# A post-norm transformer tower on one core: the scan stage's residual is added in PSUM, and the int8 stage's order on TensorE and its norms are rearranged

## The reference

```python
# L2_ffn, its last step: every expert's output goes back to the token that chose it
out = jnp.einsum('...besd,...btes->...btd', inter, perm)
...
# L3_attn
lam_t = sigmoid(x @ W.T + b);  s = lam_t * s + (1.0 - lam_t) * x
...
# L3_ffn
x_scale = jnp.maximum(jnp.abs(x2).max() / 127.0, EPS)
x_int8 = jnp.clip(jnp.round(x2 / x_scale), -128, 127).astype(jnp.int8)
out = acc_i32.astype(jnp.float32) * x_scale * weight_scale.T + bias
...
h = _layernorm(h + _L2_ffn_ref(h, ...), axis=-1)
h = _layernorm(h + _L3_attn_ref(h, ...), axis=-1)
h = _layernorm(h + _L3_ffn_ref(h, ...), axis=-1)
```

## Time and profile before

| what | value |
|---|---|
| median of 3 runs | 1355.79 us (1352.24 to 1357.06) |
| the profiled execution, its own time | 1355.12 us |
| its span | 1353.5 us |
| mean granted clock of TensorE | 0.95 |
| PE, DVE, ACT, POOL busy | 87%, 59%, 43%, 39% |
| mean DMA | 120 GB/s |

### The profile page before, as it was taken

How to read it: one execution, slowest core, us unless ns; L and a number is a source line. 1 busy time by engine, 2 the same in 40 slices (tenths; PEclk the granted TensorE clock), 3 DMA queues, 4 the chain that set the end, 5 groups by cost and what they waited for, 6 DMA issues and landing times. The chain is left out here.

```text
span 1353.5 us, 25791 instructions
## 1 busy us (share of the span) xinstructions
PE 1179.8 (87%) x9651; PEld 925.3 (68%) x9651; DVE 803.3 (59%) x1850; ACT 582.2 (43%) x1467; POOL 521.6 (39%) x564
## 2 busy tenths in 40 slices
PE   6999996698999999996899999995899999889854
PEld 4666665698999999862455656564677777667533
DVE  4666666321221221377999999994677777522886
ACT  3445542211112122155777777771343444334544
POOL 0111111232333333245688888881212212020757
PEclk9999999799999999999899999997999999889975
DMA  4111100888888888389000000002000040037601
GB/s 143 42 48 40 41 13 13 308 336 346 321 323 330 314 331 322 93 217 249 1 1 1 1 1 1 1 1 82 13 10 13 10 192 1 2 125 266 184 5 59
DMA packets 82716, 162.31 MB, mean 120 GB/s; under 512 B 42976, under 2 KB 61536, under 8 KB 76576
## 3 DMA queue, kind: packets, MB, share of 16 engines
q1 hardware_dynamic: 63504, 114.38, 24.8%
q0 software_dynamic: 10224, 44.05, 8.4%
q10 hardware_dynamic: 8864, 2.23, 0.8%
HBM read 134.28 MB, written 26.35 MB: 119 GB/s over the span
## 5 line engine op out<-in xcount | busy, mean ns | idle before, releaser
L936 PE MATMUL banks<-rowsT,w_up 128*128 128x128 f32 x1716 | 201.8, 278 | 0.2 <-DMA w_up<-in_up_w 0.2
L936 PEld LDWEIGHTS banks<-rowsT,w_up 128*128 128x128 f32 x1716 | 198.6, 195 | 0.5 <-DMA w_up<-in_up_w 0.4
L1457 PEld LDWEIGHTS banks<-ys,ident 128*128 128x128 f32 x1008 | 127.7, 191 | 99.5 <-POOL ys L1837 65.6
L1834 POOL TENSOR_TENSOR ys<-xT_d,q_by_time 128x1024 f32<-128x1024 f32 x63 | 149.3, 2370 | 40.5 <-ACT xT_d L1589 40.5
L1457 PE MATMUL banks<-ys,ident 128*128 128x64 f32 x1008 | 136.3, 290 | 21.5 <-POOL ys L1837 21.4
L1448 PE MATMUL banks<-made,ident 128*128 128x512 f32 x256 | 138.2, 622 | 10.7 <-DVE made L1772 10.5
L1670 ACT ACTIVATE banks<-banks,rate 128x256 f32<-128x256 f32 x256 | 104.0, 444 | 71.9 <-DVE made L1767 71.5
L1105 DVE TENSOR_TENSOR hT<-banks,silu 64x128 f32<-64x128 f32 x39 | 11.0, 283 | 168.3 <-ACT silu L993 168.3
L950 PE MATMUL banks<-w_down,hT 128*128 128x256 f32 x468 | 107.5, 379 | 0.6 <-DVE res L1115 0.6
L878 POOL DMA_DIRECT2D w_down<-in_down_w x39 | 22.6, 579 | 189.8 <-PE banks L950 181.7
L1770 DVE TENSOR_REDUCE banks<-made 128x32 f32<-128x544 f32 x128 | 93.1, 727 | 4.4
(11 more groups left out here) (316 smaller groups left out, 2393.9 us busy)
## 6 DMA issues: line engine op xcount, KB each, us to landing
w_up<-in_up_w SPq DMA_DIRECT2D x39, 1408.0 KB, 6.0
w_down<-in_down_w POOLq DMA_DIRECT2D x39, 768.0 KB, 5.3
inter<-res_x SPq DMA_DIRECT2D x16, 512.0 KB, 3.0
back<-inter SPq DMA_DIRECT2D x15, 512.0 KB, 3.8
patches<-in_patches SPq DMA_DIRECT2D x16, 384.0 KB, 3.3
f<-in_f SPq DMA_DIRECT2D x6, 1024.0 KB, 10.3
ys<-token_rows SPq DMA_DIRECT2D x16, 256.0 KB, 2.8
xn_rows<-xn_all SPq DMA_DIRECT2D x16, 128.0 KB, 1.7
```

Of the source, the lines that this page charges most:

```text
L936: ins = pe.matmul(out[:, m * P:(m + 1) * P], w[:, c, m * P:(m + 1) * P], x[:, c, :], start=(c == 0), stop=(c == 1))
L1457: ins = pe.matmul(o_sum[t % 2], ident[:, :], products[t % 2][:, :, :, n], start=(n == 0), stop=(n == FOLDED - 1))
L1834: pool.tensor_tensor(qs[:, :, :, :], Sc[(t + 1) % 2][:, :, :, :], bcast(qt[:, t, :, :], 2, HD), ALU.mult).then_inc(sem("qs_made"), 1)
```

## The change

Five edits, all in `last_layers`.

1. In `mix_back`, TensorE first multiplies the tile of `H` with the identity into the PSUM bank; the four mixing matmuls then accumulate on it (`start=False`). VectorE's add (`r1`) goes. Statistics and first norm read the PSUM bank. The bank is free for tile t only once the first norm of tile t - 2 has been done.
2. On TensorE, the int8 stage's list is now `turn_q`, `int_sums`, `turn_v`; `turn_v` was first.
3. Odd tiles' third norm: GpSimd makes only root and shift, ScalarE the norm (`odd_third_norm`, at lag 3, last in its tick). Even tiles stay on GpSimd.
4. The semaphore `ln3_done` becomes `third0` and `third1`, one for each parity.
5. The wait for the residual's semaphore moves from `statistics` to its callers.

```diff
                 for t in range(T):
-                    sp.wait_ge(sem("ln3_done"), t + 1)
+                    sp.wait_ge(sem(f"third{t % 2}"), t // 2 + 1)
                     sp.dma_start(io["out"][t * P:(t + 1) * P, :], res_q[t % 2][:, :]).then_inc(sem(f"out{t % 2}"), 16)
...
                     if t >= 2:
-                        pe.wait_ge(sem("added1"), t - 1)
+                        pe.wait_ge(sem("ln1_done"), t - 1)
+                    pe.matmul(mixed_bank(t), ident[:, :], H[:, t, :], start=True, stop=False, skip_group_check=True)
                     for k in range(GPT // 2):
                         at = slice(k * 2 * GROUP, (k + 1) * 2 * GROUP)
-                        ins = pe.matmul(mixed_bank(t)[at, :], perm_t[:, t, at], back[t % BACKS][:, k, :], start=True,
+                        ins = pe.matmul(mixed_bank(t)[at, :], perm_t[:, t, at], back[t % BACKS][:, k, :], start=False,
                                         stop=True, skip_group_check=True, tile_position=(0, k * 2 * GROUP))
...
-                ticks([(2, turn_v), (0, turn_q), (1, int_sums)], 2)
+                ticks([(0, turn_q), (1, int_sums), (2, turn_v)], 2)
...
-                    normed(1, x[t % 4][:, :], r1, t)
+                    normed(1, x[t % 4][:, :], mixed_bank(t), t)
...
+                def odd_third_norm(t):
+                    if t % 2:
+                        act.wait_ge(sem("ln3_shift"), t // 2 + 1)
+                        if t >= 3:
+                            act.wait_ge(sem("out1"), 16 * (t // 2))
+                        act.activation(res_q[1], r3[1][:, :], ACT.Identity, bias=shift[3][1][:, :],
+                                       scale=agg[3][1][:, 1:2]).then_inc(sem("third1"), 1)
...
-                ticks([(0, copy_qT), (1, dequantize)], 1)
+                ticks([(0, copy_qT), (1, dequantize), (3, odd_third_norm)], 3)
...
                 def third_norm(t):
                     root(3, t)
+                    if t % 2:
+                        if t >= 3:
+                            pool.wait_ge(sem("third1"), t // 2)
+                        pool.tensor_scalar(shift[3][1][:, :], agg[3][1][:, 0:1], agg[3][1][:, 1:2], -1.0,
+                                           ALU.mult, ALU.mult).then_inc(sem("ln3_shift"), 1)
+                        return
...
                 def add_back(t):
                     dve.wait_ge(sem("mixed_back"), t + 1)
-                    if t >= 2:
-                        dve.wait_ge(sem("ln1_done"), t - 1)
-                    dve.tensor_tensor(r1[t % 2][:, :], mixed_bank(t), H[:, t, :], ALU.add).then_inc(sem("added1"), 1)
-                    statistics(1, r1, t)
+                    statistics(1, mixed_bank(t), t)
...
                 def add_int(t):
                     dve.wait_ge(sem("v_turned"), t + 1)
                     if t >= 2:
-                        dve.wait_ge(sem("ln3_done"), t - 1)
+                        dve.wait_ge(sem(f"third{t % 2}"), t // 2)
```

More of the change, by code:

```diff
@@ L2327, in last_layers @@
         agg = {n: [sb(f"agg_{n}{p}", [P, 2]) for p in range(2)] for n in (1, 2, 3)}
-        shift = {n: [sb(f"shift_{n}{p}", [P, 1]) for p in range(2)] for n in (1, 2)}
+        shift = {n: [sb(f"shift_{n}{p}", [P, 1]) for p in range(2)] for n in (1, 2, 3)}
         largest = sb("largest", [P, T])
@@ L2546, in normed @@
                     act.wait_ge(sem(f"ln{n}_shift"), t + 1)
-                    act.activation(dst, r[t % 2][:, :], ACT.Identity, bias=shift[n][t % 2][:, :],
+                    act.activation(dst, r, ACT.Identity, bias=shift[n][t % 2][:, :],
                                    scale=agg[n][t % 2][:, 1:2]).then_inc(sem(f"ln{n}_done"), 1)
@@ L2571, in second_norm @@
                 def second_norm(t):
-                    normed(2, H[:, t, :], r2, t)
+                    normed(2, H[:, t, :], r2[t % 2][:, :], t)
                 def copy_qT(t):
@@ L2628, in third_norm @@
                     root(3, t)
+                    if t % 2:
[4 more added lines that the diff above has]
+                        return
                     if t >= 2:
-                        pool.wait_ge(sem(f"out{t % 2}"), 16 * (t // 2))
+                        pool.wait_ge(sem("out0"), 16 * (t // 2))
                     pool.tensor_scalar(res_q[t % 2][:, :], r3[t % 2][:, :], agg[3][t % 2][:, 0:1],
-                                       agg[3][t % 2][:, 1:2], ALU.subtract, ALU.mult).then_inc(sem("ln3_done"), 1)
+                                       agg[3][t % 2][:, 1:2], ALU.subtract, ALU.mult).then_inc(sem("third0"), 1)
                 for b in (*xT, *lam, *y):
@@ L2653, in statistics @@
                 def statistics(n, r, t):
-                    dve.wait_ge(sem(f"added{n}"), t + 1)
-                    dve.bn_stats(stats[n][t % 2][:, :], r[t % 2][:, :]).then_inc(sem(f"ln{n}_stats"), 1)
+                    dve.bn_stats(stats[n][t % 2][:, :], r).then_inc(sem(f"ln{n}_stats"), 1)
                     dve.wait_ge(sem(f"ln{n}_stats"), t + 1)
@@ L2674, in add_scanned @@
                                              op0=ALU.mult, op1=ALU.add).then_inc(sem("added2"), 1)
-                    statistics(2, r2, t)
+                    dve.wait_ge(sem("added2"), t + 1)
+                    statistics(2, r2[t % 2][:, :], t)
                 def scan(t):
@@ L2702, in add_int @@
                     if t >= 2:
-                        dve.wait_ge(sem("ln3_done"), t - 1)
+                        dve.wait_ge(sem(f"third{t % 2}"), t // 2)
                     dve.tensor_tensor(r3[t % 2][:, :], scanned_bank(t), H[:, t, :], ALU.add).then_inc(sem("added3"), 1)
-                    statistics(3, r3, t)
+                    dve.wait_ge(sem("added3"), t + 1)
+                    statistics(3, r3[t % 2][:, :], t)
                 for q in range(QUADS):
```

## The result

| | before | changed |
|---|---|---|
| median | 1354.34 us (7 runs, 1352.12 to 1360.81) | 1363.94 us (7 runs, 1361.29 to 1367.13) |
| ratio | | 1.0053, 95% interval 1.0031 to 1.0075 |
| span of the profiled execution | 1353.5 us | 1360.9 us |
| mean granted clock of TensorE | 0.95 | 0.945 |

The changed kernel is slower, by 7.2 us at the ratio (4 to 10 us by the interval). The medians are 9.6 us apart. The prediction was 1364.8 us. The spans differ by 7.4 us, and two stages account for it.

What follows compares the result with a forecast made beforehand. It took VectorE to bound the scan stage and a TensorE-ScalarE loop the int8 stage. Int8 stage +12.1 and scan stage -3.1 gave +9.0 us, so 1364.8 us against the median of 1355.8, range 1359.5 to 1370.

Steps and rivals of the forecast that it cites:

- The int8 loop: Int8 stage: a TensorE-ScalarE loop of 2.22 us gives way to a serial round of VectorE and TensorE, +13.7 us.
- The forecast of the tick: Int8 stage: six pieces from add to add sum to 3.27 us against 2.22, in 13 intervals.
- The last two intervals between adds: End of the int8 stage: with nothing left to quantise they take 3.0 us instead of 4.3, -1.3 us.
- The ends of the int8 stage: Behind the last add: shift and ScalarE's norm stand in for GpSimd's norm of 1.23 us, -0.3 us.
- The odd norms: Int8 stage: odd tiles' norms on ScalarE cost nothing and bring nothing apart from the shorter end.
- The scan stage: TensorE becomes the bound at 2.93 us a tick, VectorE's falls from 3.33 to 2.88; -3.1 us in all.
- the rule of the Trainium skill: Scan stage: statistics from PSUM cost VectorE some 0.065 us more, so the stage brings 0.2 us less.
- Ten ticks: Steady scan stage: the tick falls by 0.40 us over a stretch of 33.3 us, -4.0 us.
- The start of the scan stage: Ahead of the first `lam_logits`: uncovered `H` matmul at clock 0.50 costs 2 x 0.46, +0.9 us.
- The first: Int8 stage: `turn_q` never waits for VectorE, tick 1.87 us, kernel faster at 1347.8 us; chance 0.06.
- The second: Int8 stage: TensorE's clock is granted in full, tick 2.72 us, total 1357.6 us; chance 0.05.
- The third: Scan stage: matmul of `H` costs 0.86 us or more, the stage gains nothing, total 1368.8 us; chance 0.12.

Runs made afterwards that it cites:

- e3: Kernel before with only the odd third norms moved to ScalarE and the semaphore split by parity; ratio 1.0002 to the kernel before.
- e6: Changed kernel with VectorE's add one tick later (lag 3 for 2) and `turn_v` first again on TensorE; ratio 0.9947 to the kernel before.
- e2: Kernel before with only TensorE's int8 order changed (`turn_v` last); ratio 1.0079 to the kernel before.
- e4: Changed kernel with VectorE's add one tick later in its list (lag 3 for 2); ratio 0.9926 to the kernel before.
- e8: Changed kernel with the matmul of `H` issued twice for each tile; ratio 1.0108 to the kernel before.
- e1: Kernel before with only the residual added by TensorE in PSUM; ratio 0.9966 to the kernel before.
- e5: Changed kernel with only TensorE's int8 order undone (`turn_v` first again); ratio 0.9964 to the kernel before.
- e7: Changed kernel with VectorE's add one tick later and all third norms on GpSimd again; ratio 0.9933 to the kernel before.
- e9: Changed kernel with six more identity matmuls ahead of `turn_q` from the fourth tile on; ratio 1.0018 to the kernel before.
- e10: The kernel of e6 timed once more, without a further edit; ratio 0.9954 to the kernel before.

## Why the prediction was right, and where it was off

**The int8 loop.** Right, and by the step that mattered. The bound before was the loop of `turn_v`, `turn_q`, copy and dequantising; e3 shows that it was not GpSimd, and e6 that it was this loop. The changed order makes a serial round of VectorE and TensorE; e2 shows it alone, e4 shows that opening it removes it. The forecast of the tick was 3.27 us, the measurement 3.22. The pieces: add to quantising 1.21 us as forecast, quantising 0.67 for 0.66, hand-over 0.06 for 0.05, `turn_q` 0.18 for 0.21, `int_sums` 0.43 for 0.42, `turn_v` 0.67 for 0.72. `turn_v` came out cheaper because behind `int_sums` it is recorded with 0.63 us and not 0.69. Thirteen ticks of 0.05 us are the 0.7 us by which this stage was put too high. The last two intervals between adds took 3.0 us, as forecast.

**The ends of the int8 stage.** The last add to the end of the span: -0.4 us, where -0.3 was forecast.

**The odd norms.** Forecast at nothing, measured 1.0002 in e3.

**The scan stage.** TensorE took over as the bound, as forecast: tick 2.90 for 2.93, since the matmul costs 0.43 us (e8) and not 0.46. The statistics from PSUM took 0.42 us and those from SBUF 0.43, so the row was the better guide than the rule of the Trainium skill that I weighed against it ("VectorE: DVE Perf Modes", the section on the TRN2 errata), by which they would have been 0.065 us longer.

Ten ticks, from the third scan to the thirteenth, took 33.3 us before and 29.4 now, -3.9 us where -4.0 was forecast. The first of the ten took 3.5 us, with a scan of 1.05 us in it, and the others 2.87 to 2.90, while VectorE caught up with TensorE. The three ticks behind them took 0.1 us more.

**The start of the scan stage.** This was the step that failed: I put +0.9 us on the first `H` matmuls, at the clock of 0.50 that the profile of before shows there, and took it that the clock would be 0.50 there with the change too. It was 1.00. From the first matmul to the third scan it took 14.5 us before and 13.9 now, so -0.6 where +0.9 was forecast. These 1.5 us, less 0.1 in the ten ticks and 0.1 behind them, are the 1.3 us by which the stage's forecast (-3.1 for a measured -4.4) was off. The runs show why. From the first matmul to the first scan it was 9.4 us before and 9.2 in e3, with the clock down to 0.50 on the way, but 7.9 in e2, which has the same scan stage and the clock at 1.00 all through. The stretch of e2 that answers to the first of the earlier trace rows (columns as there):

```profile
1257.60:1259.60 2.00, 2.00 (x26) 1.31 (x21) 1.19 (x4) 1.31 (x4) 1.09 (x4) 1.00 0.84 253
```

With one `H` matmul for each tile it was 8.3 us in the changed kernel, e1, e4, e5, e6, e7, e9 and e10, and with two 9.6 in e8, with the clock at 1.00 in every one. So up to the first scan the single matmuls cost 0.5 us at an equal clock, and a clock that does not fall gives back 1.3 to 1.6. Up to the third scan they cost 0.5 to 1.0 (13.5 to 14.0 us against 13.1 in e2); executions of the same stage differ by that much. The sum of 0.9 would have been near, had the clock been the same in both; that it changed was not in the forecast. TensorE's wait ahead of the first `turn_x` is 1.1 us now and was 1.94; in e2 it is 1.3. That the matmul of `H` is what keeps the clock up is likely (down in two of three profiles without it, in none of nine with it), but no run tested it alone.

**The nearness of the total.** It is partly luck. From the start of the scan stage to the end the change took 6.9 us more where 9.0 was forecast. Both terms were too high, by 0.7 and 1.3 us. The medians, each of seven executions that scatter over 9 and 6 us, happen to lie 9.6 us apart. Had the clock not fallen in the profile of before, its stretch would be about 1.6 us shorter (9.4 against 7.9), and the change would cost some 8.5 us by this estimate.

**The rivals.** The first (order helps, 1347.8) was wrong for the change, but the tick that it named is there to be had: e4's is 1.84 us on the average, where it said 1.87, and e4 lands at 0.9926, which is 1344.3 us on a median of 1354.3. The second (full clock, tick 2.72) was wrong for the change and right in its price: e9 measured 2.71. The third (the matmul of `H` dear, 0.86 us) fell with e8, where one costs 0.43.

## What to carry to other kernels

Where engines run through fixed lists with lags, a step moved within a tick changes which loop closes: before moving one, write down for every wait which step releases it and what stands ahead of that step on its own engine, all the way round. An engine named by the chain of waits is the bound only if it has no idle time in the steady tick; GpSimd had 0.3 us, and halving its norms brought nothing. And when one list is reordered, the lists that feed it usually need a lag to match: the same order lost 12 us with the old lag of VectorE's add, and with a lag of one more it gained 5 to 6 (e7 and e4).

## What the runs showed of the hardware that was not expected

- The granted clock of TensorE was worth more than the work that kept it up. Filling TensorE's idle time made the int8 stage faster: at a granted clock of 1.00 instead of 0.50 its tick fell from 3.22 to 2.71 us (e9), while TensorE was busy 23.9 of 31.0 us, 132 of its 232 records there being matmuls of no use.
- The same start of the scan stage ran at a clock of 0.50 in two profiles and 1.00 in another (before, e3 and e2), worth 1.3 to 1.6 us. A price read in such a stretch belongs to one execution.
- Executions of one kernel spread with their mean granted clock. The 28 of the kernel before that ran beside e5 to e8 took 1358.6 to 1363.8 us at a clock of 0.946 or less, and 1352.0 to 1357.3 at 0.951 or more. A median can move by some us with how many executions have which clock.
- The scan instruction takes 0.70 us as a rule, but longer when it starts while GpSimd's step of x (`y<-xT_e`, 0.61 us) is running, and the longer the more of that step is left: 1.05 us with 0.49 us left (1262.15 in the changed kernel), 1.06 with 0.50 (1259.24), and 0.86 in ten ticks in a row of e8 with 0.31 left. Beside GpSimd's root, which also runs while it does, it keeps its 0.70. No run moved that step alone.
- The first step of the quantising on VectorE takes 0.34 us, and 0.43 to 0.45 in every tick in which GpSimd's norm of 1.22 us is running (each other tick of e4, almost every one of e7). The add and the statistics beside the same norm keep their 0.42 and 0.43.
